# Four graph layers on one core: TensorE's program without loops, the other engines' programs with theirs

## What is computed

```
h = maximum(layernorm(x), 0);  x = x + L0(h, adj)   # attention, 12 heads, adj added to the scores, output projection
h = maximum(layernorm(x), 0);  x = x + L1(h, adj)   # two rounds of bilinear attention (left/right products), linear part, norm
h = maximum(layernorm(x), 0);  x = x + L2(h, adj)   # two rounds: softmax(h h^T) * adj, three projections (left, self, right), norm
h = maximum(layernorm(x), 0);  x = x + L3(h, adj)   # attention, 12 heads, edges with adj <= 0 masked
```

## Time and profile before

| what | value |
| --- | --- |
| median of 3 runs | 2835.5 us (2833.78 to 2835.51) |
| profiled execution: its own time, its span | 2832.26 us, 2830.4 us |
| TensorE's mean granted clock | 0.979 of full speed |
| PE busy | 2698.6 us, 95% of the span |
| DVE, ACT, POOL busy | 1771.4, 1249.9, 1092.4 us |
| matmuls, and as many weight loads | 29,582 |
| loop turns on PE: l0, l1, l2, l3 | 13, 7, 13, 13 |
| instruction packets on queue q8 | 59, 0.97 MB |

### The profile page before, as it was taken

One profiled execution on the slowest core, in us unless ns is written; L12 is line 12 of the kernel. 1 busy time (PEld: TensorE's weight loads), 2 busy tenths in 40 slices (PEclk: granted clock), 3 DMA queues, 4 the chain that ended last, 5 costly groups with the idle time before them and its releaser, 6 DMA issues. The chain is left out here.

```text
span 2830.4 us, 75501 instructions
## 1 busy us (share of the span) xinstructions
PE 2698.6 (95%) x29582; PEld 2340.6 (83%) x29582; DVE 1771.4 (63%) x4003; ACT 1249.9 (44%) x2180; POOL 1092.4 (39%) x1081
## 2 busy tenths in 40 slices
PE   6999999977999999999959999999999969999998
PEld 5888888866888888888848888888888868888887
DVE  6777777754545545554446787787877765566564
ACT  3444444434444444444423343343343325565564
POOL 1433433332322322332232443544444443545455
PEclk9999999998999999999979999999999989999999
DMA  4222222124112212211121111111111112222221
GB/s 138 72 70 70 69 66 65 58 72 126 32 56 78 67 33 67 77 31 56 49 89 36 49 61 39 56 55 49 50 50 49 49 52 72 85 92 73 89 84 59
DMA packets 186658, 183.15 MB, mean 65 GB/s; under 512 B 79568, under 2 KB 186064, under 8 KB 186576
## 3 DMA queue, kind: packets, MB, share of 16 engines
q1 hardware_dynamic: 186576, 181.99, 20.8%
HBM read 131.61 MB, written 50.33 MB: 64 GB/s over the span
## 5 line engine op out<-in xcount | busy, mean ns | idle before, releaser
L52 PE MATMUL l_psW<-w_hi,l_hT_hi 128*128 128x384 f32 x1920 | 678.0, 353 | 0.0
L52 PE MATMUL l_psW<-w_hi,l_hT_lo 128*128 128x384 f32 x1920 | 647.0, 337 | 0.0
L52 PE MATMUL l_psW<-w_lo,l_hT_hi 128*128 128x384 f32 x1920 | 644.6, 336 | 0.0
L52 PE MATMUL l_psW<-l_hT_hi,w_hi 128*128 128x512 f32 (+1 forms) x1242 | 490.7, 395 | 12.9 <-ACT l_m L1236 3.9
L52 PE MATMUL l_psW<-l_hT_hi,w_lo 128*128 128x512 f32 (+1 forms) x1242 | 469.6, 378 | 0.0
L52 PE MATMUL l_psW<-l_hT_lo,w_hi 128*128 128x512 f32 (+1 forms) x1242 | 468.8, 377 | 0.0
L52 PEld LDWEIGHTS l_psW<-w_hi,l_hT_hi 128*128 128x128 f32 x1920 | 361.8, 188 | 34.4 <-issue 24.6
L52 PEld LDWEIGHTS l_psW<-w_lo,l_hT_hi 128*128 128x128 f32 x1920 | 362.6, 189 | 0.7
L52 PEld LDWEIGHTS l_psW<-w_hi,l_hT_lo 128*128 128x128 f32 x1920 | 361.3, 188 | 0.0
L52 PEld LDWEIGHTS l_psW<-l_hT_hi,w_hi 128*128 128x128 f32 x1242 | 235.7, 190 | 75.9 <-issue 22.1
L284 POOL TENSOR_TENSOR l_s_d<-l_s_b,l_mx 128x768 f32<-128x768 f32 x128 | 188.7, 1474 | 240.2 <-DVE l_mx L562 185.4
(11 more groups left out here) (160 smaller groups left out, 5137.5 us busy)
## 6 DMA issues: line engine op xcount, KB each, us to landing
after_l<-l_xr SPq DMA_DIRECT2D x192, 192.0 KB, 1.9
l_xl<-after_l SPq DMA_DIRECT2D x47, 768.0 KB, 4.6
l_xr<-after_l SPq DMA_DIRECT2D x32, 768.0 KB, 4.5
l_xl<-in_x SPq DMA_DIRECT2D x16, 768.0 KB, 5.2
l_xr<-in_x SPq DMA_DIRECT2D x64, 192.0 KB, 2.4
l_xr<-after_l SPq DMA_DIRECT2D x64, 192.0 KB, 2.3
out_x<-l_xr SPq DMA_DIRECT2D x64, 192.0 KB, 2.0
l_adj<-in_adj SPq DMA_DIRECT2D x48, 128.0 KB, 2.4
```

Source lines behind the costliest of these rows:

```text
L52: last = nc.tensor.matmul(out, lhs[a](c), rhs[b](c), start=(m == 0), stop=(m == n - 1))
```

## The change

TensorE's four loops are written out in Python, so each of the 46 loop turns stands in the program by itself with constants in its waits. DVE, ACT, POOL and SP keep their loops and their registers. No matmul, transfer or wait on a semaphore's value is added, removed or put at another place in the order.

```diff
@@ -197,11 +197,15 @@
-    def turns(engine, turn):
+    def turns(engine, turn, unrolled=False):
 
         turn(0, True, True, True)
-        with engine.Fori(1, last - 1) as i:
-            turn(i, False, True, True)
+        if unrolled:
+            for i in range(1, last - 1):
+                turn(i, False, True, True)
+        else:
+            with engine.Fori(1, last - 1) as i:
+                turn(i, False, True, True)
         turn(last - 1, False, True, False)
         turn(last, False, False, False)
@@ -934,7 +938,7 @@
-            turns(pe, projected_turn)
+            turns(pe, projected_turn, unrolled=True)
@@ -955,7 +959,7 @@
-            turns(pe, plain_turn)
+            turns(pe, plain_turn, unrolled=True)
@@ -1576,7 +1580,7 @@
-        with pe.Fori(0, last) as i:
+        for i in range(last):
             turn(i, True)
         turn(last, False)
@@ -2287,7 +2291,7 @@
         def loop(turn):
-            with pe.Fori(0, last) as j:
+            for j in range(last):
                 turn(j)
```

## The result

Over 20 runs each, the changed kernel takes 2837.94 us in the median (2835.39 to 2840.5) and the kernel before 2833.69 us (2830.76 to 2835.92). The ratio is 1.0015, with a 95% interval of 1.0009 to 1.0022: some 4.2 us slower, where 1.0 us faster was forecast. That is inside the 0.2% named beforehand, but the interval excludes both the forecast and no change at all. The forecast of 2834.5 us was counted from a median of 2835.5 over three runs, 1.8 us above that of the 20. The profiled execution has a span of 2835.2 us, against 2830.4.

A forecast was written before the change was run, and what follows sets the result against it. PE was taken to bound the kernel; 34 places at 0.03 us gave a 1.0 us gain, 2832.3 to 2831.3 us, and with 3.2 us from profiled execution to median, 2834.5 us. The range was 2828 to 2841 us.

The forecast's parts named there:

- What bounds, and the branches: All phases: PE bounds, busy 2698.6 of 2830.4 us; removing loop edges and registers in l3 and l2 gives 0.
- Fetching: Straight code needs about 240 instruction packets where there are 59; fetched ahead, they cost PE 0, at most 171 us.
- Rival 1: Straight turns in l0, l2 and l1 are quicker through PE's own program: 6.6 us gained, 2828 us; chance 0.08.
- Rivals 2 and 3: Second: taken branches stall on fetching, 52 us gained, chance 0.02. Third: PE starves for instructions, 44 us lost, chance 0.10.
- l0: Second `out_transposes`, 13 places: PE's start behind DVE falls from 0.13 to 0.05 us, 0.03 us each surviving.
- the 0.08 us: Cost of a register instruction carrying a just-in-time wait, taken from l1's transposes: load 0.13 us after ACT against 0.05.
- the 0.03 us of the transposes: l1's transposes waiting for ACT, 14 places: the gain taken to survive to the unit's end at each.
- 7 more before l1's `context`: Seven places in l1 where a register instruction carries the last wait, counted as gaining 0.03 us each.
- All other register instructions and all edges: 0: Everywhere outside the 34 counted places, removing PE's register instructions and loop edges changes the time by 0.
- l2: Two units stay at 51.38 us, gain 0; the 0.24 us shorter pair behind the loop was put to DVE's missing statistics.
- PE's busy time: Whole kernel: expected not to change from 2698.6 us; a change would show the prediction wrong.
- The sum: 34 places in l1 and l0 at 0.03 us: 1.0 us gained, bounds 0 and 2.7; everything else 0.

The follow-up runs named there:

- the kernel that has 145 of the added packets: Changed kernel with l1's loop on TensorE put back, l0, l2 and l3 still written out: 2834.33 us beside 2833.35, ratio 1.0001.

## Why the prediction was wrong

- **What bounds, and the branches.** TensorE bounds (busy for 2702.7 of 2835.2 us), and the removed branches and register instructions gave nothing in l3 (29.70 us) and nothing by themselves in l2: right.
- **Fetching.** 236 packets for the forecast 240, at no cost: right, and shown on its own by the kernel that has 145 of the added packets and a ratio of 1.0001.
- **Rival 1** (the straight turns' shorter periods were PE's own): wrong. With all of l2 straight, the pairs in the middle stay at 51.43 us and the last at 51.15.
- **Rivals 2 and 3** (branches that stall, TensorE starved for instructions): neither came, with l3's turn at 29.70 us in both kernels. Rival 1's 2828 us is a slip, by the way: 2835.5 less 6.6 is 2829.
- **l0.** 0.05 us behind DVE as forecast, and more of the 0.08 us survived: 0.7 us in all instead of 0.4.
- **l1, the step that failed.** It is not the 0.03 us of the transposes: 14 places gave back 0.5 us where 14 x 0.03 = 0.4 had been forecast. It is the rest of the sum: "7 more before l1's `context`" counted as a gain, and "All other register instructions and all edges: 0". Both take for granted that a constant in a wait leaves the waits where they were, and so does the description of the change, that no wait is put at another place: true of the source, not of the built program. The seven contexts lost 0.01 us each (1.01 to 1.025 us from context to context), and the other 21 in the loop, put at 0 without a row, lost 0.26. The premise was never held against l1's straight contexts. The interval from 1366.97 serves for the transposes, but it begins with unit 28, the last one of the loop, so its contexts are loop code. The only full straight interval, 1391.67 to 1416.63, is 24.96 us and stands in no comparison of the prediction, and the three loop units of 24.69 us, with which it would have shown the 0.26, neither. The row was there: in the kernel before, at the second context of its first straight unit,

```profile
1399.43 0.56 DVE L1347 TENSOR_TENSOR l_lin<-l_psW,l_b_lin 128x384 f32<-128x384 f32 x1 [1.00 <-PE l_psW L52]
...
1400.35 0.24 PEld L1538 LDWEIGHTS l_psC<-l_lin,l_delta 64*64 64x64 f32 x8 [0.82 <-issue]
```

  0.36 us from DVE's end to the load, as in the changed kernel's unit above (0.33 in the other two straight units), where units 2 to 4 of a loop turn have 0.07.
- **l2**, put at 0, lost 0.05 us a turn for the same reason: `left_set`, which comes last, had been on the load and now stands on a wait instruction before it. Moved back to the load, in the kernel with all padding left out, it returns 0.04 us of the 0.05.
- **PE's busy time**, which was to stay, rose from 2698.6 to 2702.7 us, a sign that the prediction had named for being wrong. It isn't more work, with 29,582 matmuls in both; the context's matmuls count 56.1 us instead of 53.8, at the same 507 ns each, since the two contexts overlap less (in the unit above the second's first matmul started 0.11 us before the first's last one ended, and now starts 0.18 us behind it). Where the rest of the 4.1 us comes from wasn't followed up.
- **The sum** came out as -0.7 (l0), +4.9 (l1), +0.6 (l2), 0 (l3), where -0.4, -0.6, 0 and 0 had been forecast. That the total is still within 0.2% of the forecast says nothing for it: the sign was wrong, and no rival had the mechanism, a wait that takes another place among the instructions around it.

## What to carry to other kernels

Where several waits stand before a matmul, write the one that comes last so that it is on the matmul's own load, and look for it in the built program and not in the source: in this kernel each instruction left behind it cost 0.11 us every time, and a wait instruction of its own instead of the load 0.09. Turning register waits into constants moved `lin_set` here from the last wait instruction to the first, so a straight copy of this loop was not the loop without its branch; compare each place of the body with its own straight counterpart, all of them, before the difference is called nothing. Written out with the waits in that order, this kernel takes 2828.5 us, ratio 0.9976 to the kernel before (0.9967 to 0.9986), and most of that gain needs l1 alone.

## What was not expected of the hardware

- A satisfied wait wasn't free behind a late one, at a place where the weight loads had been idle for 0.53 us in the kernel before: each wait instruction after the late one cost TensorE 0.11 us (0.81, 0.92 and 1.025 us from context to context with none, one and two), although their own records are 51 ns long, as the rows of the changed kernel's padding say:

```profile
L1469 PEldq EVENT_SEMAPHORE  x95: 51/51/51, 677.2 to 1452.2; - x95
```

- Two waits in one instruction weren't equal: with the late one second, the instruction is on record for 2213 ns and the load follows DVE by 0.07 us; with the late one first or alone, it is on record for 51 ns behind DVE's end and the load follows by 0.12 us.

- Four times as much program for TensorE, 3.87 MB of it in 236 packets, ran beside 182 MB of data without a measurable cost, also in l0 and l3, where 96 small matmuls and their loads go through in 1.6 us.
